# A state-space and mixture-of-experts layer on one core: memsets ahead of the last unused tile, a table load behind the stage, two additions of x moved into a gap

## What is computed

```python
xn = _layernorm(x)
# branch 1: state space
u = xn @ W_x.T + b_x;  g = sigmoid(xn @ W_g.T + b_g)
h = depthwise_conv(u, conv_w, kernel 3) + conv_b
u = u * g + h * (1 - g)
dt = clip(softplus(xn @ W_dt.T + b_dt).mean(axis=(0, 1)), 0.001, 2.0)
A_d = exp(-softplus(A_raw) * dt);  B_d = (A_d - 1) / (A + 1e-06) * B_ssm
new = A_d * carry + B_d * u_t          # scan over the 256 steps, 256 channels x 16 states
y_t = sum over states of new * C_ssm
attn = _layernorm(xn + y @ W_out.T + b_out) * ln_g + ln_b
# branch 2: experts; expert h = int(xn[0] + xn[1]) mod 8 and the next one, each with weight 1/2
ffn = 0.5 * sum over the two of relu(xn @ W1[e] + b1[e]) @ W2[e] + b2[e]
out = x + attn + ffn
```

## Time and profile before

| | us |
|---|---|
| median of 3 runs | 476.51 |
| lowest, highest | 476.04, 476.83 |
| profiled execution | 476.49 |
| its span, first to last instruction | 474.7 |

### The profile page before, as it was taken

One profiled execution on the slowest core, in us unless ns is written; L12 is line 12 of the kernel. 1 busy time (PEld: TensorE's weight loads), 2 busy tenths in 40 slices (PEclk: granted clock), 3 DMA queues, 4 the chain that ended last, 5 costly groups with the idle time before them and its releaser, 6 DMA issues. The chain is left out here.

```text
span 474.7 us, 11677 instructions
## 1 busy us (share of the span) xinstructions
PE 419.2 (88%) x3387; PEld 369.6 (78%) x3387; DVE 393.9 (83%) x666; ACT 315.9 (67%) x898; POOL 241.4 (51%) x272
## 2 busy tenths in 40 slices
PE   1047999998998899999999999899998999799991
PEld 1035788886998899999999999799997555478881
DVE  6989676775649999999999999899981459994997
ACT  2686799998776667777665567465666666426873
POOL 4595777777423223333263244643321777776730
PEclk9999999999899989999999999999999999989997
DMA  9997334523121121212231234422112818188544
GB/s 235 260 412 265 103 116 131 164 81 107 52 55 33 33 44 33 44 39 46 65 67 35 42 92 122 101 67 50 39 40 44 223 49 225 52 230 225 161 128 133
DMA packets 111417, 52.78 MB, mean 111 GB/s; under 512 B 48880, under 2 KB 106392, under 8 KB 111384
## 3 DMA queue, kind: packets, MB, share of 16 engines
q1 hardware_dynamic: 106328, 43.48, 35.2%
q0 software_dynamic: 4096, 8.40, 5.8%
q10 hardware_dynamic: 960, 0.52, 0.4%
HBM read 28.12 MB, written 24.25 MB: 110 GB/s over the span
## 5 line engine op out<-in xcount | busy, mean ns | idle before, releaser
L1444 PE MATMUL PS<-AR 128*128 128x128 f32 x1184 | 140.4, 277 | 4.2 <-ACT AR L766 4.2
L1444 PEld LDWEIGHTS PS<-AR 128*128 128x128 f32 x1184 | 137.1, 194 | 5.0 <-ACT AR L766 5.0
L766 ACT ACTIVATE AR<-PS,VC 128x256 f32<-128x256 f32 x296 | 112.2, 489 | 4.7 <-PE PS L1432 4.0
L1430 PE MATMUL PS<-XT,RR 128*128 128x256 f32 x296 | 86.5, 292 | 3.6 <-POOL XT L579 3.4
L1431 PE MATMUL PS<-XT,RR 128*128 128x256 f32 x296 | 83.3, 281 | 0.0
L1432 PE MATMUL PS<-XT,RR 128*128 128x256 f32 x296 | 83.3, 281 | 0.0
L579 POOL TENSOR_TENSOR XT<-XTF,XT 128x256 fp32r<-128x256 f32 x35 | 33.9, 969 | 91.4 <-ACT XT L743 91.4
L573 POOL DMA_INDIRECT sorted_tokens<-RA,posi x64 | 62.2, 971 | 23.7 <-DMA sorted_tokens<-RA,posi 11.3
L603 POOL TENSOR_TENSOR AR<-AR,b2p 128x256 f32 x37 | 36.1, 975 | 56.2 <-ACT AR L779 53.2
L779 ACT ACTIVATE AR<-PS 128x128 f32 x74 | 16.4, 274 | 68.6 <-PE PS L1444 66.2
L1430 PEld LDWEIGHTS PS<-XT,RR 128*128 128x128 f32 x296 | 56.3, 190 | 5.1 <-POOL XT L579 4.7
(11 more groups left out here) (230 smaller groups left out, 859.5 us busy)
## 6 DMA issues: line engine op xcount, KB each, us to landing
sorted_tokens<-AR SPq DMA_DIRECT2D x10, 512.0 KB, 5.7
XSIN<-sorted_tokens SPq DMA_DIRECT2D x160, 32.0 KB
sorted_outputs<-AR SPq DMA_DIRECT2D x37, 128.0 KB, 1.9
RA<-in_L_attn_x_dram SPq DMA_DIRECT2D x8, 512.0 KB, 8.1
normalised_tokens<-RA SPq DMA_DIRECT2D x16, 256.0 KB
RB<-normalised_tokens SPq DMA_DIRECT2D x8, 512.0 KB, 6.9
AR<-in_L_ffn_W_dram SPq DMA_DIRECT2D x15, 256.0 KB, 3.2
out_dram<-RB SPq DMA_DIRECT2D x7, 512.0 KB, 3.3
```

The lines of the kernel that those rows point to most:

```text
L766: nc.scalar.activation(HID[n][:, k, :], ps[2 * n + k // 2][:, (k % 2) * FT:(k % 2 + 1) * FT], ACT.Relu, bias=B1C[:, e, k:k + 1]).then_inc( ...
L1430: T.matmul(bank, W1h[slot][:, w], XT[:, 0:FT], start=True, stop=False)
L1444: ins = T.matmul(ps[5 + h][:, 0:D], HID[n][:, k, h * P:(h + 1) * P], W2S[slot][:, k, :], start=(n == 0 and k == 0), stop=(n == 1 and k == ...
```

## The change

Four edits. The two memsets now stand ahead of the transposition of tile 39, so `s_mat` no longer waits for its load. ScalarE's table load stands behind the last eviction of the state-space stage. `add_x(3)` leaves duo 14 and `add_x(4)` leaves its place behind `add_base(2)`; both now follow `y_piece(1, 4)`, ahead of `scale_batch(0)`. For that the fourth batch of x needs another home: `XTF` and `XSIN` become halves of one tile `XTX`, which holds `XB[3]` when the tiles are through; its load waits for the last transposition (`s_tt` at `NTT`), and `y_piece(0, 7)` waits for no addition.

```diff
-        XTF = sb("XTF", [P, 2 * FT])
+        XTX = sb("XTX", [P, 4 * FT])
+        XTF, XSIN = XTX[:, 0:2 * FT], XTX[:, 2 * FT:4 * FT]
...
-        XSIN = sb("XSIN", [P, 2 * FT])
...
-        XB = [batch(RC[:, 1, :], NB8 - NAR + n) for n in range(NAR)] + [batch(RB[:, 0, :], n) for n in range(NB8 - NAR)]
+        XB = [batch(RC[:, 1, :], NB8 - NAR + n) for n in range(NAR - 1)] + [batch(XTX[:, :], 0)] + [batch(RB[:, 0, :], n) for n in range(NB8 - NAR)]
...
             sp.wait_ge(s_mat, 1)
-            for n in range(NAR):
+            for n in range(NAR - 1):
                 load_x(n)
+            sp.wait_ge(s_tt, NTT)
+            load_x(NAR - 1)
...
-            nc.scalar.preload_act_table_set("natural_log_exp_and_others")
             act.wait_ge(s_mat, 1)
             decay(0)
             decay(1)
...
+            nc.scalar.preload_act_table_set("natural_log_exp_and_others")
...
-            tiles_to(MAXT + 1)
+            tiles_to(MAXT)
 
             dve.wait_ge(s_re[0], bounds[E] * KB)
             for n in range(2):
                 ins = V.memset(ps[n][:, :].rearrange("p (b c) -> p b c", c=NC)[:, :, 0], 0.0)
             ins.then_inc(s_mat, 1)
+            tiles_to(MAXT + 1)
...
-                if hb == 0 and n >= NB8 - NAR:
+                if hb == 0 and NB8 - NAR <= n < NB8 - 1:
                     dve.wait_ge(s_xb, n - (NB8 - NAR) + 1)
...
-            XQ = (DPB - 3, DPB + 1, DPB + 4, DPB + 6)
+            XQ = (DPB - 3, DPB + 1, DPB + 4)
...
             y_piece(1, 4)
+            add_x(3)
+            add_x(4)
             scale_batch(0)
...
             add_base(2)
-            add_x(4)
             y_piece(1, 7)
```

## The result

| | before | after |
|---|---|---|
| median of 9 runs each | 476.51 us (474.26 to 479.50) | 471.65 us (470.68 to 473.50) |
| profiled execution | 476.5 us | 472.0 us |
| its span | 474.7 us | 470.2 us |
| mean granted clock of TensorE | 0.982 | 0.986 |

The ratio of after to before is 0.9908, with a 95% interval of 0.9882 to 0.9933. The forecast was 472.2 us with a span of 470.4. Both came out within 0.6 us.

A forecast was written before the change was run, and what follows sets the result against it. TensorE bounds the stage until y pieces fill VectorE, and runs the output stage without a pause. Gains of 1.6 + 1.1 + 1.6 = 4.3 us take 476.5 to 472.2 us; own bounds 471.6 to 472.9, with rivals 471.0 to 474.0.

The forecast's parts named there:

- Part 1: Boundary from expert loop to state-space stage: memsets and table load moved together start the first readout 1.6 us earlier (1.4 to 2.07).
- The first addition of x: In the stage, after the eighth gather: at worst it delays the next scan by 1.0 us, costing TensorE nothing.
- Part 2: Last duo of the stage: without the fourth addition the last scan comes 1.1 us earlier (1.0 to 1.2).
- Part 3: Behind the stage's last wait: with 0.8 us left, TensorE's clock stays up, saving 1.6 us (0 to 1.6).
- rival (a): TensorE's clock falls all the same behind the remaining 0.8 us wait or the stage's 1.07 us one: 473.8 us, chance 0.15.
- Part 4: VectorE's 6.76 us hole ahead of the first statistics covers both moved additions, with 1.3 us left: cost nothing.
- Rival (d): A late x load turns VectorE's hole into a wait, from landing 10 us after issue; at 17 us 479, chance 0.03.
- Part 5: Output stage: moving the fifth addition out of VectorE's full stretch gains 0, since VectorE waits for ScalarE at 456.79.

The follow-up runs named there:

- memsets_only_2: Kernel before with only the two memsets moved ahead of tile 39, repeated on another chip; 475.31 us, ratio 0.9989.
- table_only_2: Kernel before with only ScalarE's table load moved behind the last eviction, repeated on another chip; 476.84 us, ratio 1.0016.
- add3_only: Kernel before with only the fourth addition of x and its buffer moved as in the change; 473.89 us, ratio 0.9945.
- warm_matmuls_2: Kernel before with two added unread matmuls in TensorE's wait for the stage's last scan, repeated on another chip; 474.75 us, ratio 0.9968.
- memsets_and_table_2: Kernel before with both memsets and table load moved, additions of x unmoved, repeated on another chip; 475.64 us, ratio 0.9974.
- x4_load_last: Kernel after with the load of x for the fifth addition put last in its queue; 476.21 us, ratio 0.9984 to before.
- add4_only: Kernel before with only the fifth addition of x moved into the hole ahead of the first statistics; 476.68 us, ratio 0.9990.
- memsets_only: Kernel before with only the memsets moved ahead of tile 39, on the chip where before took 515.57 us; 517.71 us.

## Why the prediction was right

**Part 1, the start.** The forecast was a scan at 365.6 and a readout at 366.9, 1.6 us earlier. They stand at 365.56 and 366.82, so the readout is 1.68 us earlier on the clock of the trace. Measured from the projection's end it is 1.85, and 1.79 to 1.83 in the three other kernels with both edits (2.91 to 2.95 us). This is the fairer measure, because tile 39 does not arrive at a fixed time: in all ten profiles of these kernels its load is issued 1.67 to 1.70 us behind the start of the last expert projection, so a later loop brings a later tile. Counted so, the forecast's 366.9 - 363.76 = 3.14 us was 0.25 too long. Tile 39 was transposed from 1.26 us behind the projection's end instead of 1.37, the scan started 0.08 us ahead of the listed end of that transposition instead of 0.02 behind it, and the rest is rounding. The upper bound of 2.07 was not reached because the scan is tied to tile 39 by VectorE (365.64), and the lower of 1.4 was too careful. `memsets_only_2` and `table_only_2` show that neither edit gives this alone.

**The first addition of x.** The prediction left its gather open and bounded it. In after the addition did wait 0.91 us for the gather, and the next scan followed it; TensorE read that scan only at 384.72:

```profile
380.61 1.22 DVE L1240 TENSOR_TENSOR AR<-AR,RC 128x1024 f32<-128x1024 f32 x1 [0.91 <-DMA AR<-sorted_outputs,posi]
381.76 1.21 DVE L1249 TENSOR_TENSOR_SCAN AR<-AR,PS 128x512 f32<-128x512 f32 x1
```

The forecast had the scan end at 383.7 at worst; it ended at 382.97, and nothing waited.

**Part 2, the fourth addition.** 1.1 was booked and 1.20 measured from first to last readout, 1.15 in `add3_only`; the remaining wait was forecast at 0.8 and is 0.79.

**Part 3, the clock.** 1.6 was booked and 1.62 measured, in after, in `add3_only` and in `warm_matmuls_2`, which changes nothing else there. The size is shown. The condition was put too simply: I reasoned that a shorter wait keeps the clock up, and gave rival (a) 0.15 for a fall all the same. It did not come in three profiles with 0.8 us. But `memsets_and_table_2` shows that the old wait did not always cost the 1.6 us, so in some executions of before this term probably has nothing to give. The Trainium skill (TensorE: Matmul & The Clock Gate, Part 1) calls the hardware's window free-running, and by that the same wait can end either way; the pair `table_only_2` and `memsets_and_table_2` agrees with it.

**A term that the sum lacks.** Closing the hole at the boundary also removes a place where the clock can fall. In the profile of before it did not fall there, so I saw nothing to price. It fell there in two of five kernels with the hole. In `warm_matmuls_2` it cost 6.28 - 4.74 = 1.5 us, in `table_only_2` 5.90 - 4.74 = 1.2 ahead of the first readout and 47.59 - 47.14 = 0.45 behind it, together 1.6. That may be a part of why the runs of before spread over 5.2 us and those of after over 2.8, and why the medians of all runs differ by 4.86 us where the profiled executions differ by 4.5. No profile exists of the single runs, but the mean granted clock of each is on record. Of the 35 runs of before at a median of 476.87 us, the six with 0.985 or more took 473.4 to 476.0 us, the 18 with 0.981 or 0.982 took 474.7 to 477.3, and the eleven with 0.979 or less took 477.5 to 479.8. Their median is 0.981, that of the nine runs of after 0.988, while the two profiled executions have 0.982 and 0.986. So the times go with the clock. At which wait it fell in a single run stays open, and the expert loop adds a spread that the change does not touch: it ends between 362.05 and 366.27 in the ten profiles.

**Luck in the number.** The two profiled executions that the forecast was made from and is held against have the same two falls in the expert loop, at 119.5 and 167.3, and their loops end within 0.17 us of each other. So the sum of 4.3 us against 4.5 could show its fit; against other pairs of profiles the same mechanism would have stood up to 4 us off. The mechanism rests on the stretches in the table, not on this. The forecast's own upper bound of 472.9 does not come from its terms: with the clock staying up, their lower bounds, 1.4 + 1.0 + 1.6 = 4.0, give 472.5.

**Part 4, the hole.** Booked at nothing with 1.3 us left, and 1.52 us were left. The x of the fifth addition landed 8.7 us after the issue, where 8.6 was taken from before. Rival (d), which needed a landing past 10 us, did not occur, and `x4_load_last` shows that its mechanism is real: with the refinement 6.43 us late, the end was 4.53 us late. The prediction passed the whole delay on to the end and set the point where the gain is gone at 14 us (14.3 by its numbers). In `x4_load_last` the x landed 16.6 us behind the first issue of that queue, which by this rule gives 476.5 + 16.6 - 14.3 = 478.8 us; the median was 476.21 and the profiled execution 477.67. The prediction did not count the 1.9 us that are made up behind the refinement.

**Part 5, the fifth addition.** Booked at nothing, and `add4_only` gives 0.01 us in the trace and a ratio of 0.9990. The tie to ScalarE, not VectorE's full row, was the right thing to go by.

## What to carry to other kernels

When two engines each stand in the way of a start, price the edits together and then each alone: here they gave 1.85 us together, and 0.4 and 0 alone. An engine that is full to the end is not the bound if a tie to another engine stands further on; what is taken from ahead of the tie returns as a wait at it. A wait of TensorE of about 2 us costs more than its length on average, since it can also bring a fall of the clock behind it that costs 1.5 to 1.6 us, and one profile does not tell whether it does: compare several.

## What the runs showed of the hardware

The same wait, of 1.92 and 1.93 us in the same place, was followed by a granted clock of 0.50 in one kernel and of 1.00 in another, whose code from the first duo on is the same. Waits of 0.79 or 0.80 us there were never followed by a fall, in three profiles, nor was any wait of 0.7 to 1.71 us elsewhere in the ten.

One chip ran the kernel before at 515.57 us instead of 476 to 477, and in `memsets_only` there waits on VectorE are ended by no instruction that the profile names (22.6 us at one line), and TensorE pauses for 0.76 and 0.82 us around the readout matmuls of one duo, which nothing in the profile explains.

The 512 KB loads of one queue do not land alike: in `x4_load_last` the median of the four in the output stage is 8.7 us from issue to landing, as for the first of them in after, and the one put last took 10.2. That is the place in the queue rather than the new order: the last of the four took 9.7 us in after too, 9.7 to 10.2 in seven of the ten profiles and 8.6 to 8.7 in before, `memsets_only_2` and `table_only_2`. What makes the difference is open.
